# A graph network kernel: the bias column g by row sums on VectorE, edge keys without a mask, two load queues, a new written order

## The reference: two layers over 1024 nodes and 33,792 edges

```
h = relu(layernorm(x))                       # x: 1024 x 512
q = h @ Wq + bq;  k = h @ Wk + bk;  v = h @ Wv + bv
adj[src, dst] = 1
a = (q @ k.T / sqrt(512)) * adj + (1 - adj) * -1e6
x = x + softmax(a) @ v
h = relu(layernorm(x))
agg = segment_sum(h[src], dst) / max(deg, 1)
x = x + alpha * (agg @ W.T + b)
```

## Time and profile before

| what | us |
|---|---|
| median of three runs | 240.35 (240.06 to 240.42) |
| the profiled execution | 240.38 |
| its span, first to last instruction | 238.6 |
| PE busy | 232.7 (98%) |
| VectorE busy | 163.4 (68%) |
| ScalarE busy | 80.8 (34%) |
| GpSimd busy | 71.5 (30%) |

### The profile page before, as it was taken

How to read it: one execution, slowest core, us unless ns; L and a number is a source line. 1 busy time by engine, 2 the same in 40 slices (tenths; PEclk the granted TensorE clock), 3 DMA queues, 4 the chain that set the end, 5 groups by cost and what they waited for, 6 DMA issues and landing times.

```text
span 238.6 us, 3313 instructions
## 1 busy us (share of the span) xinstructions
PE 232.7 (98%) x1296; PEld 188.5 (79%) x1296; DVE 163.4 (68%) x282; ACT 80.8 (34%) x147; POOL 71.5 (30%) x104
## 2 busy tenths in 40 slices
PE   7999799999999999999999999999999999999995
PEld 5476489788888888888888888888888888888885
DVE  6999999998979482885749975757574263064222
ACT  3299972843222132233260623232342002060000
POOL 4187172000000019971431643434153306000000
PEclk9999999999999999999999999999999999999999
DMA  6990000000000001040000000000000000001232
GB/s 210 332 371 17 1 3 0 0 3 0 0 3 26 18 3 47 3 140 36 0 0 3 0 0 0 3 0 1 0 0 3 0 0 0 3 3 44 94 122 92
DMA packets 5616, 9.41 MB, mean 39 GB/s; under 512 B 864, under 2 KB 1376, under 8 KB 5600
## 3 DMA queue, kind: packets, MB, share of 16 engines
q1 hardware_dynamic: 4880, 8.91, 10.5%
q10 hardware_dynamic: 720, 0.28, 0.4%
HBM read 7.09 MB, written 2.10 MB: 39 GB/s over the span
## 4 chain that ended last, share of the span: by engine, by line
PE 86%; DVE 10%; DMA 2%; issue 0%; ACTq 0%; DVEq 0%
PE bank L804 22%; PE bank L806 21%; PE bank L805 21%; PE bank L953 12%; PE bank L825 5%; DVE ohW L553 3%; DVE ohL L549 3%; PE bank L973 3%; DMA src_i<-in_src 2%; DVE hT_lo L604 1%; DVE M_lo L634 1%; PE bank L864 1%; PE bank L889 0%; PE bank L851 0%; DVE key_b L540 0%
## 5 line engine op out<-in xcount | busy, mean ns | idle before, releaser
L804 PE MATMUL bank<-V_hi,pT_hi 128*128 128x512 f32 x64 | 25.6, 401 | 0.0
L422 ACT ACTIVATE h2f<-xs,nmr,rstd 128x512 f32<-128x512 f32 x8 | 6.5, 816 | 56.3 <-POOL nmr L365 56.3
L549 DVE TENSOR_TENSOR ohL<-iotaL,lo_b 128x1024 bf16<-128x1024 bf16 x33 | 22.6, 686 | 4.0 <-PE bank L825 4.0
L553 DVE TENSOR_TENSOR ohW<-iotaW,key_b 128x1280 bf16<-128x1280 bf16 (+4 forms) x33 | 25.2, 763 | 0.0
L804 PE MATMUL bank<-hT_hi,GT_hi 128*128 128x512 f32 x64 | 25.1, 392 | 0.0
L806 PE MATMUL bank<-V_hi,pT_lo 128*128 128x512 f32 x64 | 25.0, 391 | 0.0
L806 PE MATMUL bank<-hT_hi,GT_lo 128*128 128x512 f32 x64 | 25.0, 390 | 0.0
L953 PE MATMUL bank<-A,h_hi 128*128 128x512 f32 x64 | 24.9, 389 | 0.0
L953 PE MATMUL bank<-A,h_lo 128*128 128x512 f32 x64 | 24.9, 389 | 0.0
L805 PE MATMUL bank<-hT_lo,GT_hi 128*128 128x512 f32 x64 | 24.9, 389 | 0.0
L805 PE MATMUL bank<-V_lo,pT_hi 128*128 128x512 f32 x64 | 24.9, 389 | 0.0
(11 more groups left out here) (135 smaller groups left out, 528.2 us busy)
## 6 DMA issues: line engine op xcount, KB each, us to landing
xs<-in_x SPq DMA_DIRECT2D x4, 512.0 KB, 9.2
out_dram<-o_sb SPq DMA_DIRECT2D x7, 256.0 KB, 2.0
wq_raw<-in_wqT SPq DMA_DIRECT2D x4, 256.0 KB, 6.4
wk_raw<-in_wkT SPq DMA_DIRECT2D x4, 256.0 KB, 7.1
wv_raw<-in_wv SPq DMA_DIRECT2D x1, 1024.0 KB, 12.7
wt_raw<-in_wT SPq DMA_DIRECT2D x1, 1024.0 KB, 5.4
bv_sb<-in_bv SPq DMA_DIRECT2D x1, 256.0 KB, 3.3
b_sb<-in_b SPq DMA_DIRECT2D x1, 256.0 KB, 3.1
```

The lines of the kernel that those rows point to most:

```text
L422: nc.scalar.activation(out, xs[:, t, :], ACT.Relu, bias=nmr[:, layer, t:t + 1], scale=rstd[:, layer, t:t + 1]).then_inc(relu, 1)
L549: nc.vector.tensor_tensor(ohL[:, q % RING, :, :].rearrange("p b (m two) -> p b m two", two=2), bcast(iotaL[:, :].rearrange("p (m two) -> p ...
L553: nc.vector.tensor_tensor(ohW[:, q % RING, :, 0:row].rearrange("p b (m two) -> p b m two", two=2), bcast(iotaW[:, 0:row].rearrange("p (m t ...
L804: mm(out, lhs[0][a], rhs[0][b], start=(first and k == 0), stop=False)
```

## The change

- **g without PE.** wk is loaded a second time in its natural rows (`wk_rows`, 1 MB), bq as one row copied to all partitions (`bq_row`). Both loads stand behind wv on SP's queue. gsum is now four multiply-and-sum instructions of 128x512 on VectorE, each waiting for the one before, and the last one releases `g0`. Step g is gone on PE and on VectorE.
- **Keys without the mask.** The mask and its minimum are gone. ScalarE converts `lo_b` and sums what lies below or above the window by two Relu activations with an accumulator; the bb step has a second one-column matmul for it and no longer a minimum. The constant 1 of the key moves into the window's start.
- **bqk_s and bprod** are made by GpSimd instead of VectorE.
- **Two queues.** ScalarE issues wk0 ahead of dst; SP issues src in wk0's old place.
- **Order.** All orders are new, GpSimd has its own.

```
-PE_ORDER = ("Mk0 Mk1 c1 bb c2 M0 c2 T0 c1 M1 T1 c1 T2 c1 M2 c1 M3 c1 T3 c2 G0 T4 G1 G2 g c2 T5 c1 G3 T6 T7 u c3 G4 G5 G6 c3 "
-           "V0 c3 V1 V2 V3 c2 G7 V4 c2 V5 c2 V6 V7 c3")
+PE_ORDER = ("Mk0 Mk1 bb c3 M0 c2 T0 c1 M1 c2 T1 M2 M3 T2 T3 c3 G0 G1 G2 G3 T4 u c3 V0 T5 V1 c3 V2 V3 T6 V4 V5 c3 T7 V6 c3 "
+           "G4 G5 c3 G6 c2 G7 c2 V7 c3")
-DVE_ORDER = ("o4 bb o4 T0 o3 T1 T2 M0 o1 M1 M2 M3 T3 gsum o1 usum o2 T4 g wv0 o2 G0 T5 o1 T6 G1 T7 G2 o2 dot0 dot1 G3 dot2 "
...
+DVE_ORDER = ("o3 bb o5 T0 o2 T1 M0 o1 M1 M2 M3 T2 T3 gsum wv0 o2 wv1 G0 usum o1 G1 o1 G2 dot0 o1 dot1 G3 o1 u dot2 T4 T5 V0 "
...
-                for raw, w_d, loaded in ((wq_raw, wqT_d, ld_wq), (wk_raw, wkT_d, ld_wk)):
-                    sp.dma_start(raw[:, k, :], w_d[k * P:(k + 1) * P, :]).then_inc(loaded[k], 16)
+                sp.dma_start(wq_raw[:, k, :], wqT_d[k * P:(k + 1) * P, :]).then_inc(ld_wq[k], 16)
+                if k == 0:
+                    sp.dma_start(src_i[:, :], src_d).then_inc(ld_edges, 16)
+                else:
+                    sp.dma_start(wk_raw[:, k, :], wkT_d[k * P:(k + 1) * P, :]).then_inc(ld_wk[k], 16)
...
+            sp.dma_start(wk_rows[:, :, :], wk_d.rearrange("(k p) n -> p k n", p=P)).then_inc(ld_g, 16)
+            sp.dma_start(bq_row[:, :], bqrow_d.partition_broadcast(P)).then_inc(ld_g, 16)
...
+            act.dma_start(wk_raw[:, 0, :], wkT_d[0:P, :]).then_inc(ld_wk[0], 16)
             act.dma_start(dst_i[:, :], dst_d).then_inc(ld_edges, 16)
-            act.dma_start(src_i[:, :], src_d).then_inc(ld_edges, 16)
...
+            act.wait_ge(src_low, 1)
+            nc.scalar.activation(lo_b[:, :, :], bcast(key_i[0][:, :], 2, 2), ACT.Copy).then_inc(tables, 1)
+            act.wait_ge(past, 1)
+            nc.scalar.activation(stray[:, 0, :], key_t[0][:, :], ACT.Relu, bias=1.0, scale=-1.0,
+                                 accum_out=bprod[:, KD:KD + 1]).then_inc(strays, 1)
...
-                nc.vector.tensor_copy(lo_b[:, :, :], bcast(key_i[0][:, :], 2, 2))
...
-                link(nc.vector.tensor_tensor(key_t[2][:, :], key_t[0][:, :], wide[:, :], ALU.is_lt))
-                link(nc.vector.scalar_tensor_tensor(out=key_t[3][:, :], in0=key_t[0][:, :], scalar=0.0,
-                                                    in1=key_t[2][:, :], op0=ALU.is_ge, op1=ALU.mult))
-                link(nc.vector.scalar_tensor_tensor(out=key_t[1][:, :], in0=key_t[1][:, :], scalar=1.0, in1=key_t[0][:, :],
-                                                    op0=ALU.add, op1=ALU.add))
-                link(nc.vector.tensor_tensor(key_b[:, :, :], bcast(key_t[1][:, :], 2, 2), bcast(key_t[3][:, :], 2, 2), ALU.mult))
-                nc.vector.tensor_reduce(bprod[:, KD:KD + 1], key_t[3][:, :], AX.X, ALU.min)
-                dve.wait_ge(tables, 2)
+                nc.vector.tensor_tensor(key_b[:, :, :], bcast(key_t[1][:, :], 2, 2), bcast(key_t[0][:, :], 2, 2), ALU.add)
+                nc.vector.tensor_tensor(key_t[2][:, :], key_t[0][:, :], wide[:, :], ALU.subtract).then_inc(past, 1)
+                dve.wait_ge(tables, 3)
+                dve.wait_ge(past, 1)
...
+                    dve.wait_ge(ld_g, 32)
+                    for m in range(KD):
+                        if m:
+                            dve.wait_ge(g_dots, m)
+                        nc.vector.tensor_tensor_reduce(
+                            out=g_scr[:, :], in0=wk_rows[:, m, :], in1=bq_row[:, :], scale=SCALE, scalar=0.0, op0=ALU.mult,
+                            op1=ALU.add, accum_out=g0[:, m:m + 1]).then_inc(g_kept if m == KD - 1 else g_dots, 1)
...
-                elif step == "g":
-                    pe.wait_ge(g_sum, 1)
-                    pe.wait_ge(hT_lo, KD)
-                    for m in range(KD):
-                        last = mm(bank[7][:, m:m + 1], t_g[:, m * P:(m + 1) * P], f(ones_r[:, 0:1]), start=True, stop=True)
-                    last.then_inc(g_ps, 1)
```

More of the change, by code:

```diff
@@ L119, in steps, with gnn_kernel @@
     return out
-PE_STEPS, ACT_STEPS, DVE_STEPS = steps(PE_ORDER), steps(ACT_ORDER), steps(DVE_ORDER)
+PE_STEPS, ACT_STEPS, DVE_STEPS, POOL_STEPS = (steps(order) for order in (PE_ORDER, ACT_ORDER, DVE_ORDER, POOL_ORDER))
 PROJ = [s for s in PE_STEPS if s[0] in ("M", "u", "G", "V")]
 NPROJ = len(PROJ)
-def gnn_kernel(nc, x_d, src_d, dst_d, wqT_d, wkT_d, wv_d, wT_d, bq_d, bk_d, bv_d, b_d, alpha_d, out_d):
+def gnn_kernel(nc, x_d, src_d, dst_d, wqT_d, wkT_d, wk_d, bqrow_d, wv_d, wT_d, bq_d, bk_d, bv_d, b_d, alpha_d, out_d):
     with ExitStack() as ctx:
@@ L163, in gnn_kernel @@
         wk_raw = place("wk_raw", [P, KD, D], F32, r_G + 8 * KB)
-        g_terms = place("g_terms", [P, 2, D], F32, r_G + 16 * KB)
         u_terms = place("u_terms", [P, 2, D], F32, r_V + 24 * KB)
-        t_g, t_u = g_terms[:, 1, :], u_terms[:, 1, :]
+        t_u = u_terms[:, 1, :]
+        wk_rows = place("wk_rows", [P, KD, D], F32, r_V + 16 * KB)
+        bq_row, g_scr = (place(n, [P, D], F32, r_V + (28 + 2 * i) * KB) for i, n in enumerate(("bq_row", "g_scr")))
         V = [place("V_hi", [P, NT, D], F32R, r_V), place("V_lo", [P, NT, D], F32R, r_V + 16 * KB)]
@@ L187, in gnn_kernel @@
         win0 = place("win0", [P, ET], F32, r_W2 + 2 * KEY)
-        key_t = [place(f"key_t{i}", [P, ET], F32, r_W2 + (3 + i) * KEY) for i in range(4)]
+        key_t = [place(f"key_t{i}", [P, ET], F32, r_W2 + (3 + i) * KEY) for i in range(3)]
         wide = place("wide", [P, ET], F32, r_W2 + 9 * KEY)
@@ L373, in _ @@
             pool.wait_ge(consts, 5)
-            for step, n in ACT_STEPS:
+            pool.wait_ge(ld_bqk, 32)
+            link(nc.gpsimd.tensor_scalar(bqk_s[:, :, :], bqk[:, :, :], SCALE, None, ALU.mult))
+            nc.gpsimd.tensor_tensor(bprod[:, 0:KD], bqk_s[:, 0, :], bqk[:, 1, :], ALU.mult).then_inc(vec_ready, 1)
+            for step, n in POOL_STEPS:
                 if step == "sum":
@@ L583, in _ @@
                     nc.vector.tensor_reduce(bb[:, :], bank[7][:, 0:KD], AX.X, ALU.add).then_inc(bb_kept, 1)
-                elif step in ("gsum", "usum"):
-                    weights, raw, terms, done = (0, wk_raw, g_terms, g_sum) if step == "gsum" else (1, wq_raw, u_terms, u_sum)
+                elif step == "gsum":
+                    dve.wait_ge(ld_g, 32)
[5 more added lines that the diff above has]
+                            op1=ALU.add, accum_out=g0[:, m:m + 1]).then_inc(g_kept if m == KD - 1 else g_dots, 1)
+                elif step == "usum":
+                    dve.wait_ge(vec_ready, 1)
@@ L593, in _ @@
                         if k < KD - 1:
                             link(ins)
-                    ins.then_inc(done, 1)
+                    ins.then_inc(u_sum, 1)
                 elif step == "wv":
```

57 lines of the change are left out of this document (29 added, 28 removed).

## The result

The changed kernel takes 238.36 us in the median of six runs (237.59 to 238.9), the kernel before 240.34 in six runs beside it (240.06 to 240.45). The ratio is 0.9913 with an interval from 0.9893 to 0.9933: 2.0 us faster. The forecast was 238.1, 2.3 us faster. The profiled execution took 237.70 us with a span of 235.8, against 240.38 and 238.6: 2.7 us less. The forecast lies between the two.

What follows compares the result with a forecast made beforehand. PE was taken to bound the kernel, busy 232.7 of 238.6 us. G0 earlier (-2.12), batch 11 behind it (+0.65) and step g gone (-0.80) sum to -2.27 us: 240.38 becomes 238.1 us, range 237.3 to 239.8.

Steps and rivals of the forecast that it cites:

- The start: PE's first product Mk0 starts at 4.5 instead of 4.99, as wk0 is issued 0.44 us earlier.
- The rival in which it starts no earlier: Mk0 stays at 4.99 because wq0 and wk0 share the transfer engines; G0 at 28.2, 238.6 us; chance 15%.
- bb and the flag: PE starts bb at 11.4; VectorE, its keys 1.7 us earlier, loses 0.65 us waiting for bb ahead of the flag.
- M0: On PE, M0's second half waits for wk3 till 14.4, a bubble of 0.3 us; M0 ends at 15.3 against 15.39.
- G0: The first large product starts at 27.7, 2.1 us earlier; the ways of PE and VectorE to it both end at 27.6.
- Batch 11 and g: Behind G0, PE gets batch 11, +0.65 us, and loses step g, -0.80 us.
- before there was 0.1 us of idle time here, so nothing can be won: In the rest to the scores, PE gains nothing; a few waits of 0.1 to 0.3 us could be lost, none taken.
- u: PE asks for u at 39.2, behind usum on VectorE at 38.7, with a cover of 0.3 to 0.5 us.
- The loads: wk_rows lands at 22.3 and bq_row at 25.6 at the latest, ahead of gsum's need at 27.4.
- The slower rival by the second load: gsum waits for the late wk_rows and bq_row, deciding from 30.5 on; landing at 31.5 gives 241.9 us; chance 8%.
- Given back later: After G0, four or five waits of 0.2 to 0.3 us cost 1.1 us: 239.2 us; chance 18%.

Runs made afterwards that it cites:

- one-queue kernel: The changed kernel with loads issued as before, wk0 second on SyncE and dst and src first on ScalarE: 238.44 us, ratio 0.9915.
- x2: The changed kernel with g made as before, by weighted sums on VectorE and four one-column products on PE, without the second wk load: 239.11 us, ratio 0.9949.
- the fifth row sum: The changed kernel with one more, unused row sum of 128x512 on VectorE ahead of the four of gsum: 239.32 us, ratio 0.9946.

## Why the prediction was right, point by point

The mechanism held: G0 comes 2.06 us earlier (2.12 forecast), with a batch more and step g less behind it. That the median of 238.36 lies so close to 238.1 is in part luck. The span fell by 2.8 us and not by 2.3, for reasons that the sum did not have, and the median lies 0.66 us above the profiled execution, by a scatter that it did not have either. The two misses point in opposite ways.

**The start.** Mk0 was put at 4.5 and came at 4.52. The rival in which it starts no earlier is not what happened: wq0 and wk0 from two queues were both there by then. The one-queue kernel shows what it would have cost, 0.58 us at G0 where 0.5 was taken, of which 0.17 is the slower Mk of that execution.

**bb and the flag.** bb was forecast at 11.4 and the flag at 11.9; they came at 11.46 and 12.00. The keys ended at 7.56 instead of 7.8, so VectorE idled 0.94 us instead of 0.65. The prediction called this a loss of 0.65 us out of 1.7 won at the keys. It missed what else it means: a chain that used to have some cover against PE now has none, and whatever varies in Mk reaches G0. That is a mechanism it did not have, and the likely source of the difference between the profile's 2.7 us and the median's 2.0.

**M0.** The step "its second half needs wk3, which lands at 14.34" failed. wk3 was issued at 5.20 and landed 8.5 us later, at 13.7, not 9.3 us after an issue at 5.04; the second half of M0 started on time and M0 ended at 14.94 instead of 15.3. It moved nothing, since PE does not set G0: it idles 0.36 us ahead of it.

**G0.** Forecast 27.7, from two chains that end at 27.6; measured 27.76 and 27.68. VectorE began batch 4 at 13.62 instead of 13.4 and its pair of low parts of T2 and T3 at 26.39, T3's at 26.98 instead of 26.8.

**Batch 11 and g.** Both terms were right. Step g is 0.80 us, as the row said, and x2 shows 0.75 to 1.0 us in all with the wait that it causes at T4. The distances between PE's matmul starts, added up by kind from G0 to the first score, give 11.71 us of counting before and 12.35 now: 0.64 for the batch, which was taken at 0.65. The sum of the two was to be -0.15; the stretch shortened by 0.46.

**The mis-sized term.** The missing 0.3 us are PE time that the records count as busy. By the same sums T4 to T7 cost 1.95 us before and 1.50 now, 0.46 less; V's matmuls cost 0.26 more, and those of G0 to G3 0.08 less. The largest single piece is a wait that no idle record of PE shows. Before, T6 and T7 took 44.44 to 45.60, 1.16 us, while two transposes of the same form stand at 0.87 us (24.15 to 25.02) in the changed kernel. From the kernel before, T7's weight loads and T5's low part on VectorE:

```profile
45.11 0.42 PEld L864 LDWEIGHTS bank<-ident,h 128*128 128x128 f32 x4 [0.31 <-issue]
```
```profile
44.31 0.68 DVE L604 TENSOR_TENSOR hT_lo<-bank,hT_hi 128x512 fp32r<-128x512 f32 x1
```

T7 writes the bank that T5's low part reads, so it waits until VectorE is done with that at 44.99. The last matmul of T6 starts at 44.76 and the first of T7 at 45.14, 0.37 us apart where 0.11 is usual. The step that erred is "before there was 0.1 us of idle time here, so nothing can be won". A busy record may hold a wait. It fits that PE's busy time fell to 231.6, where 232.1 was forecast.

**u.** It was to be asked for at 39.2 with a cover of 0.3 to 0.5 us. It started at 39.20 without a wait; by the fifth row sum the cover was 0.22, less than forecast. gsum took 30.39 - 27.58 = 2.81 us, forecast 2.8.

**The loads.** wk_rows was put at 22.3 and bq_row at 25.6 at the latest; they landed at 21.7 and 23.7. The slower rival by the second load had its point of decision at 30.5, and never came near.

**Given back later.** No new idle record of PE shows behind G0 (the first score at 87.23, forecast 87.5). The keys, which the sum counted as part of G0's gain, are worth 0.5 us in the profiled execution and nothing in the median: nine runs with masked keys have 237.94 us, ten without 238.13. The new order with the old keys would have done as well.

## What to carry to other kernels

Shortening what stands ahead of a meeting of two engines gains until the other one is waited for; from there on the kernel also takes over that engine's scatter, so compare spreads and not only medians, and take several profiles. When an order is written out by hand, price the new parts under the old order and the old parts under the new one: here the order was worth 1.1 to 1.3 us on top of the new parts, at least as much as any one of them. Where the trace says "busy throughout", compare the distance between two starts with that of the same step elsewhere before you conclude that nothing can be won there.

## What was not expected of the hardware

The rate of the first real matmuls after eight warm-up matmuls differs from one execution to the next: in some the first few were 0.86 us apart instead of 0.43, worth 0.8 us in all, while the granted clock of the profile stood at 1.00. An issue on SyncE's queue took 0.65 us for the 1 MB of wv and 2.56 us for the 1 MB of wk_rows right behind it, then 2.39 us for the 256 KB of bq_row; with some 5 MB of loads ahead of them these two issues filled SyncE from 7.68 to 12.67 us. The row sum over 512 elements cost 0.61 us and 0.12 us more for the wait between two of them.
